# An attention kernel in which a group's maxima become rows two chunks later in TensorE's order

## The reference

```python
q, k_t, v_t = heads(x @ W_q), heads(text @ W_k), heads(text @ W_v)
probs_t  = softmax(q @ k_t.T * scale)                 # text tokens
text_out = probs_t @ v_t
attn     = q @ k_ip.T * scale                         # the 4 image tokens
qsem     = l2norm(probs_t @ text)                     # per head: 512 columns more
probs_ip = softmax(attn + 0.5 * qsem @ l2norm(ip).T) * mask
x1 = (text_out + probs_ip @ v_ip) @ W_out + b_out + x
```

## Time and profile before

| | us |
|---|---|
| median of 3 runs | 3646.74 |
| lowest, highest | 3644.2, 3650.6 |
| the profiled execution | 3650.53 |
| its span in the trace | 3648.7 |
| PE busy | 3440.8 |
| DVE busy | 2018.2 |
| ACT busy | 1638.5 |
| POOL busy | 824.4 |

### The profile page before, as it was taken

How to read it: one execution, slowest core, us unless ns; L and a number is a source line. 1 busy time by engine, 2 the same in 40 slices (tenths; PEclk the granted TensorE clock), 3 DMA queues, 4 the chain that set the end, 5 groups by cost and what they waited for, 6 DMA issues and landing times.

```text
span 3648.7 us, 58131 instructions
## 1 busy us (share of the span) xinstructions
PE 3440.8 (94%) x21896; PEld 2650.6 (73%) x21896; DVE 2018.2 (55%) x4648; ACT 1638.5 (45%) x3628; POOL 824.4 (23%) x648
## 2 busy tenths in 40 slices
PE   6999999999999999999999999999999999877887
PEld 3788999997888887777777777777688877633333
DVE  4544444453444455655555565655555565656986
ACT  0233434442332345444454454444444554534876
POOL 2111000101101122222222221212221121234665
PEclk8999999999999999999999999999999999988999
DMA  4220111112252111131451111213143111139221
GB/s 157 56 82 25 50 35 28 36 27 82 53 63 71 45 52 50 33 93 36 59 98 43 46 48 50 52 32 88 39 53 37 26 32 33 25 99 79 55 52 33
DMA packets 391741, 196.67 MB, mean 54 GB/s; under 512 B 296972, under 2 KB 355164, under 8 KB 391458
## 3 DMA queue, kind: packets, MB, share of 16 engines
q1 hardware_dynamic: 391464, 192.96, 24.8%
HBM read 136.68 MB, written 55.44 MB: 53 GB/s over the span
## 4 chain that ended last, share of the span: by engine, by line
PE 81%; DVE 6%; ACT 5%; DMA 3%; issue 2%; POOL 2%; SPq 1%; POOLq 0%; ACTq 0%; DVEq 0%
PE acc L783 9%; PE acc L776 9%; PE acc L778 8%; PE acc L779 8%; PE acc L784 8%; PE acc L777 7%; PE av L817 3%; PE spare L853 3%; ACT prob L958 2%; PE spare L817 2%; PE acc L810 2%; PE acc L808 2%; PE score L741 2%; PE score L736 2%; PE score L743 2%
## 5 line engine op out<-in xcount | busy, mean ns | idle before, releaser
L958 ACT ACTIVATE prob<-score 128x512 f32<-128x512 f32 x1280 | 799.4, 625 | 1642.4 <-PE score L743 1241.7
L776 PE MATMUL acc<-tok_v,prob_hi 128*128 128x300 f32 x2240 | 873.4, 390 | 11.8 <-DVE v_f L1083 3.7
L961 ACT ACTIVATE prob_hi<-score 128x512 fp32r<-128x512 f32 x1280 | 799.9, 625 | 0.0
L783 PE MATMUL acc<-tok_v,prob_lo 128*128 128x278 f32 (+1 forms) x2560 | 746.9, 292 | 7.3 <-DVE prob_lo L1021 7.3
L778 PE MATMUL acc<-tok_lo,prob_hi 128*128 128x256 f32 (+1 forms) x2560 | 742.5, 290 | 0.0
L779 PE MATMUL acc<-tok_lo,prob_hi 128*128 128x256 f32 (+1 forms) x2560 | 720.5, 281 | 0.0
L784 PE MATMUL acc<-tok_v,prob_lo 128*128 128x256 f32 (+1 forms) x2560 | 719.5, 281 | 0.0
L1021 DVE TENSOR_TENSOR prob_lo<-prob,prob_hi 128x512 fp32r<-128x512 f32 x880 | 653.0, 743 | 96.7 <-ACT prob_hi L961 95.7
L1255 POOL TENSOR_TENSOR prob_lo<-prob,prob_hi 128x512 fp32r<-128x512 f32 x400 | 529.9, 1338 | 730.5 <-ACT prob_hi L961 729.5
L777 PE MATMUL acc<-tok_v,prob_hi 128*128 128x256 f32 x2240 | 629.2, 281 | 0.0
L778 PEld LDWEIGHTS acc<-tok_lo,prob_hi 128*128 128x128 f32 (+1 forms) x2560 | 485.3, 190 | 10.4 <-issue 9.6
(11 more groups left out here) (221 smaller groups left out, 4438.9 us busy)
## 6 DMA issues: line engine op xcount, KB each, us to landing
k_ring<-k_scr SPq DMA_DIRECT2D x480, 64.0 KB
ctx_t<-in_ctxT SPq DMA_DIRECT2D x8, 2048.0 KB, 10.8
q_ring<-q_scr SPq DMA_DIRECT2D x480, 32.0 KB
v_scr<-v_stage SPq DMA_DIRECT2D x32, 440.0 KB, 2.5
tok_v<-v_scr SPq DMA_DIRECT2D x80, 176.0 KB, 3.3
k_scr<-part_bf SPq DMA_DIRECT2D x32, 384.0 KB, 2.5
v_scr<-v_stage SPq DMA_DIRECT2D x36, 330.0 KB, 9.2
v_ring<-v_scr SPq DMA_DIRECT2D x80, 148.5 KB, 3.3
```

The lines of the kernel that those rows point to most:

```text
L776: e.matmul(out_a[:, 0:SEG + VCOLS], p_hi, tok_v[0:kk, c, seg, v_lo:v_lo + SEG + VCOLS], start=first, stop=False)
L783: e.matmul(out_a[:, v_one:v_one + SEG + VH], p_lo, tok_v[0:kk, c, seg, v_lo + v_one:v_lo + v_one + SEG + VH], start=False, stop=False)
L958: e.activation(prob[:, es, :], bank_s[:, :], ACT.Exp, scale=SCALE)
L961: e.activation(prob_hi[:, ps, :], bank_s[:, :], ACT.Exp, scale=SCALE).then_inc(s_exp, 1)
```

## The change

The task that closes a group's maxima no longer emits its step when its turn in the background queue comes. It puts it into `urgent` with a due chunk two further on (`rest=2`). Only group 0, before the first chunk, keeps the old way.

```diff
-    def maxima(g):
+    def maxima(g, rest=2):
...
         def rows_task():
             o.open_job("max_rows", g)
             o.add("max_rows", g)
-        return [half_task(j, st, half) for j in range(GROUP) for st in range(ST) for half in range(2)] + [rows_task]
+
+        def rows_later():
+            urgent.append((now[0] + rest, rows_task))
+        halves = [half_task(j, st, half) for j in range(GROUP) for st in range(ST) for half in range(2)]
+        return halves + [rows_later if rest else rows_task]
...
-    rest, top = first_v[5:], maxima(0)
+    rest, top = first_v[5:], maxima(0, rest=0)
```

## The result

| | before | after |
|---|---|---|
| median, us | 3645.5 (4 runs) | 3692.3 (4 runs) |
| ratio | 1 | 1.0126, 95% interval 1.0110 to 1.0142 |
| span of the profiled execution | 3648.7 | 3690.2 |
| PE / DVE busy, us | 3440.8 / 2018.2 | 3440.1 / 2038.3 |

The change makes the kernel 46.8 us slower; I had forecast 10 us. The sign was right, the size was not, and 3692.3 is outside the range of 3640 to 3671.

A forecast was written before the change was run, and what follows sets the result against it. TensorE was taken as the bound from 130 to 3179 us, then VectorE, ScalarE and TensorE close together. Terms -5.4 + 3.6 + 4 + 2.3 + 5.7 + 4 - 4 gave +10.2 us, forecast 3657 us, range 3640 to 3671.

The forecast's parts named there:

- group 11: Chunk 158 to 160: old wait gone, new 6.7 us wait behind the cast of token block 7, clock falls; +3.6 us.
- group 24: Chunk 370 to 372: new place behind `fuse_exp`, a wait of 3.1 us; +2.3 us.
- group 38: Chunk 593 to 595: waited for nothing, goes behind `combine` of unit 4, waits 4.0 us, clock falls; +5.7 us.
- groups 23 and 43: Ends of batches 1 and 2: new wait some 6 us, replacing 2.33 and most of a 5.27 us stand; +2 us each.
- group 58: Chunk 915 to 917: the 3.70 us wait behind `combine` and 1.7 for the clock go; -5.4 us.
- the short ones: Small waits at steps landing behind a `v` or `split`, less small waits taken away: +4 us, between 0 and +8.
- the last 16 groups: Only layer 1 left, three engines nearly equally busy: -4 us, between -14 and +4.
- five or six steady groups give about 0: Last 16 groups: VectorE, with 0.58 us idle, is as far behind at the new place, so about no gain.
- The rule for it: Two-SBUF-input VectorE and SBUF-reading GpSimd instructions exclude each other: up to 1.3 us more each at batch ends 1 and 2.
- 73 and 74 can give 1 to 4 each: Late groups 73 and 74 get a place with no `max` reduction ahead: 1 to 4 us gained each.
- 66 and 67 lose 1 to 2 each: Late groups 66 and 67 land behind a `split` with its `lower`, or a `v`: 1 to 2 us lost each.
- The SyncE rival: Late groups: rows' DMAs behind ring loads land late, TensorE waits 1 to 3 us in three or four groups; chance 0.05.

The follow-up runs named there:

- e4_steady_small: Kernel before with the step two chunks later for groups 70 to 79 and GpSimd's prob_lo subtractions cut to 64 of 512 columns from group 62: ratio 0.9959.
- e1_late: Kernel before with the step two chunks later only for groups 64 to 79: ratio 1.0052, +19 us.
- e2_sync: Kernel before with only the rows' six DMAs of the last 16 groups put behind the ring loads on SyncE: ratio 1.0054, +20 us.
- e1_early: Kernel before with the step two chunks later only for groups 1 to 63: ratio 1.0094, +34 us.
- e3_skip: Kernel before with the step two chunks later for groups 1 to 63 except 11, 23, 24, 38, 43 and 63: ratio 1.0030, +11 us.
- e3_few: Kernel before with transpose and following operations two chunks later, VectorE's neg_max reduction unmoved, for groups 4, 5, 17, 18, 38, 58, 60 only: 0.9974, -9.5 us.
- e1_neg: Changed kernel, but VectorE's reduction into neg_max keeps its old place; transpose and following operations move: ratio 1.0084 against the kernel before, +31 us.

## Why the prediction was wrong

**Right: a wait is exchanged for another, and at which places.** The total of the early transposes was to be 25 to 33 us; it is 34.1, just above. Expected and traced waits: group 11 6.7 and 6.73, group 24 3.1 and 3.20, group 38 4.0 and 3.70, groups 23 and 43 about 6, and 6.07 and 6.26, group 58 none. The terms in time: -5.4 was -4.7, +3.6 was +3.3, +2 and +2 were +1.3 and +2.2, +2.3 was +2.6, +5.7 was +4.1. The clock fell to 0.50 behind the first as assumed. These six sum to +8.8 against +10.2 (without the short ones and the late groups). That the whole forecast is +10.2 as well is chance: its last two terms, +4 and -4, cancel. The prediction's own sign of being wrong, a start of group 63 not 8 to 20 us later, came true: it is 26.4 later.

**Wrong: the short ones, +4.** They were sized by the transposes' waits only. What is left of the 26.4 us is 26.4 - 8.8 = 17.6. The short transposes alone wait 8.1 us, against 2.1 before. The larger part is another: I asked what stands ahead of the reduction on VectorE and, except at the ends of the batches, not what stands behind the split. The five operations now come closer ahead of a chunk's `prob_lo`, for which TensorE waited 13.2 us more. Of its waits 2.2 and 2.6 us are in groups 22 and 42, behind the ends of two batches, where the term had a price. New at places that had none are 1.02 us in each of groups 24, 32, 36, 40 and 44 and 1.09 in 56 and 58; in group 62 the wait is 4.06 instead of 1.09. That clearest place is the maxima of group 63, which I hadn't named. The step now stands directly ahead of `combine`, and TensorE waits at 3190.34:

```profile
3190.34 0.64 PE L814 MATMUL acc<-prob_lo,v_ring 128*33 128x512 f32 x1 [4.06 <-DVE prob_lo L1025]
```

Group 62, in which this falls, is 5.3 us longer, with the five operations beginning here on VectorE:

```profile
3182.92 0.28 DVE L1141 COPY max_t<-av 16x128 f32<-16x128 f32 x1 [1.15 <-PE av L831]
3183.23 1.14 DVE L1143 CAST max_bf<-max_t 16x128 bf16<-16x128 f32 x1
```

and here is GpSimd's subtraction at the same time, which ends at 3184.30; the cast ends at 3184.37:

```profile
3183.02 1.28 POOL L1259 TENSOR_TENSOR prob_lo<-prob,prob_hi 128x512 fp32r<-128x512 f32 x1 [2.36 <-ACT prob_hi L965]
```

**Wrong: the last 16 groups, -4.** The step of the forecast that failed is "five or six steady groups give about 0", and with it "the steady ones should keep 17.5 us with VectorE busy for 16.9". They took 19.70 and 19.13. Of the others that I meant, group 70 lost 2.5 us (of which unchanged kernels show 1.0 to 1.4) and 77 2.2, and 71, 75 and 76 lost 0.4, 1.0 and 0.3. I reckoned with VectorE's queue as a fixed amount of work. It isn't: its operations last longer where they meet GpSimd's. The rule for it stood in the prediction and was left out of the sum, priced at 1.3 us in two places only. In the steady group the step's first operation, `TENSOR_SCALAR`, meets it at once:

```profile
3445.14 1.11 DVE L1135 TENSOR_SCALAR neg_max<-max_parts 128x8 f32<-128x8 f32 x1
...
3448.70 1.43 DVE L1025 TENSOR_TENSOR prob_lo<-prob,prob_hi 128x512 fp32r<-128x512 f32 x1
...
3452.44 1.62 DVE L1025 TENSOR_TENSOR prob_lo<-prob,prob_hi 128x512 fp32r<-128x512 f32 x1
```

```profile
3443.73 2.50 POOL L1259 TENSOR_TENSOR prob_lo<-prob,prob_hi 128x512 fp32r<-128x512 f32 x2 [0.64 <-ACT prob_hi L965]
3448.29 2.96 POOL L1259 TENSOR_TENSOR prob_lo<-prob,prob_hi 128x512 fp32r<-128x512 f32 x2 [2.06 <-ACT prob_hi L965]
3452.24 1.27 POOL L1259 TENSOR_TENSOR prob_lo<-prob,prob_hi 128x512 fp32r<-128x512 f32 x1 [0.98 <-ACT prob_hi L965]
```

It begins at 3445.14 and ends at 3446.25; GpSimd's pair ends at 3446.23. The `prob_lo` of 3452.44 waits until GpSimd's ends at 3453.51 and then takes 0.55 us more, near the usual 0.67. Before, the step stood at the end of a group and such a `prob_lo` took 0.67 in most places. VectorE had 0.58 us to spare in a steady group, so 2.2 us of lengthening go straight into the time, and with GpSimd's work cut they are gone (`e4_steady_small`).

The late part of the changed kernel's trace against the one of before, by groups (us): 63 and 64 -0.9, 65 to 67 +10.5, 68 +3.8 (with the 2.58 us for the rows), 69 and 70 +4.7, 71 +0.4, 72 to 74 -4.0, 75 to 78 +2.6, and 79 -2.0; together +15.1. "73 and 74 can give 1 to 4 each" looks right in kind, with -4.0 for the maxima of 73 to 75, but 2.3 of that are in group 72, which is as short in kernels that move nothing there; 0.6 and 1.0 us are left. "66 and 67 lose 1 to 2 each" was +3.5 and +4.2; the 3.5, in group 65, is 1.1 in `e1_late`, whose late program is the same.

**The SyncE rival** was given 0.05 and 1 to 3 us in three or four groups. Its mechanism is real: 2.6 us of wait in the changed kernel, 6.3 with the order alone, +13 us from four groups. Even at a DMA share of 0.13 `e2_sync` has a wait of 0.92 us at the first score of group 77. I priced the rows by a steady stage, where the DMA share is 0.25, and not by the stage where it is 1.08 to 1.23; and it was the issue on SyncE that came late there, and not the landing. In the changed kernel it is worth about 5 us in groups 66 and 67, by the kernels with the order put back; in the total time these don't show it.

**What stays open.** What makes up the rest of the 10.5 us of groups 65 to 67, beside the about 5 us of the rows behind the loads. VectorE's longer wait for `v_stage` and a difference between executions are the two candidates. Four kernels with an unchanged program there (`e1_early`, `e3_skip`, `e3_few` and before) differ by up to 5 us in group 67. It is also open why putting the order back, which shortens these groups, brought the total only 1 and 4 us. Nor are the 12.3 us of the short ones outside group 62 accounted for place by place. Steps of 1.2 to 1.5 us at groups 24, 32, 36, 40 and 44 remain in `e1_neg` too, each with its 1 us of waiting for `prob_lo`, so they don't come from the reduction; the split's operations ahead of that `prob_lo` are the likely cause, but they were not moved by themselves.

## What to carry to other kernels

Moving a step later on every engine gives nobody a head start: the wait becomes that of the new place. Leaving the producer's part where it was took every one of the early transposes' waits away (`e1_neg`), but that kernel was still 31 us slower than before, with the consumer's other operations moved everywhere. What came out faster was a choice of seven places read from a trace (`e3_few`). When small operations are moved on a busy VectorE, look at both sides of the new place: what is queued ahead of them, who waits for what comes behind them, and what GpSimd runs at that time. And ask of every small transfer that passes behind big ones how full the DMA engines are in that stage, and when its issue can begin.

## What the runs showed of the hardware that I had not expected

- **Small one-input operations are held up as well.** I had thought of operations with two inputs. The 16x128 cast took 1.14 us instead of 0.21, and the 128x8 `TENSOR_SCALAR` 1.11 instead of 0.16, each ending within 0.07 us of GpSimd's instruction, while the `TENSOR_REDUCE` lines beside them kept their lengths. The Trainium skill counts casts, copies and `tensor_scalar` in their two-port modes among those that can exclude GpSimd, and `tensor_reduce` not (SBUF — State Buffer, section "Who interferes with whom"). The trace agrees with each of these: the copy L1179, from SBUF to SBUF, takes 0.25 us twice and 0.84 and 0.85 us twice, with GpSimd's instruction ending 0.2 us before it there.
- **The lengthening costs less time than it adds up to.** Cutting GpSimd's work from group 62 on took VectorE's lengthening behind the start of group 63 from 27 us to 2 in the kernel before, and gave 16 us.
- **The issue of six 2 KB DMAs** took 4.07 us in a steady group and 7.12 us behind the ring loads at a DMA share of 1.09; the first alone makes the difference, with 3.69 us against 0.66.
